# A two-layer state-space and expert kernel: order of TensorE's work in 28 of 47 expert tiles, and expert weights in three transfers

## The chip, the cores and the metric

One Trainium2 chip, one core of it. The metric is the device time of one execution in microseconds (us); less is better. The core's engines are TensorE (PE in the profile, its weight loads PEld), VectorE (DVE), ScalarE (ACT), GpSimd (POOL) and SyncE (SP, which here only issues transfers).

## The reference

`x` is 4 batches of 512 tokens with 512 channels. Two layers follow each other; each has a mixing part and a feed-forward part, both added to `x` with a gate:

```python
x = x + tanh(g_xattn[0]) * _L0_xattn_ref(ctx_1024, _layernorm(x), ...)   # state-space scan
x = x + tanh(g_ffn[0])   * _L0_ffn_ref(_layernorm(x), ...)               # 16 experts, 4 per token
x = x + tanh(g_xattn[1]) * _L1_xattn_ref(ctx_1024, _layernorm(x), ...)   # state-space scan
x = x + tanh(g_ffn[1])   * _L1_ffn_ref(_layernorm(x), ...)               # linear layer with low-rank experts
```

The scan keeps 16 states for each of 512 channels and goes along the 512 positions of a batch:

```python
state = state * exp(d[..., None] * A) + (d * u)[..., None] * b[:, None, :]
y = einsum('bdn,bn->bd', state, c)
```

The first layer's feed-forward part is a mixture of experts: `acc + we * (silu(x @ g.T) * (x @ u.T) @ d.T)` over 16 experts, where `g` and `u` are 256x512, `d` is 512x256 and `we` is zero for all but 4 experts of a token; a shared expert of the same shape is added. Everything is float32.

## The kernel before, in words

**Stages.** There are 8 scan stages `s`, one per layer and batch. Each has 32 units (16 states, each for two halves of the channels). A unit `k` is: ACT makes the decay (`exp`, L712), DVE multiplies (`mul_b`, L1702) and scans (L1710), POOL multiplies by C (`mul_c`, L457), and the result is summed; in stages 5 to 7 the sum is DVE's (`add_y`, L1721). The scan of the second layer does not need the first layer's output except at its end, so the expert work of the first layer is laid beside stages 5, 6 and 7 (`FIRST_B` = 5).

**Expert tiles.** The routed tokens are gathered in 47 tiles (`NTILE`), each for one expert: 32 full ones of 256 rows and 15 half ones of 128 rows (`KINDS`: tile `j` is half where `j % 3 == 1` and `j > 1`). Each of stages 5 to 7 has 16 turns (`TPS`) of two scan units, and a turn carries one tile. Turn `n` of stage `s` carries tile `j = 16 * (s - 5) + n - 1`, so tiles 0 to 14 lie in stage 5, 15 to 30 in stage 6 and 31 to 46 in stage 7. In stages 5 and 6 the turns with `n` up to 8 also carry the next stage's projection and convolution on PE (banks 4 and 5, `PRE`), and the turns up to 15 its softplus on ACT and DVE.

**One tile** has these steps: POOL gathers its rows (`gather_rows`, two turns ahead); PE transposes them (`tile_transposes`, L1164, halves `h` = 0 and 1); ACT copies them to `XST` (`tile_rows`, L762; one buffer for all tiles); PE makes gate and up products for two halves of the inner size (`tile_in`, L1185, `it` = 0 and 1, 16 matmuls each, banks 0 and 1); ACT takes the silu (`tile_silu`, L769), DVE multiplies (`tile_hidden`, L1728, which releases `h_ready`); PE multiplies by the down weights (`tile_out`, L1196, `it` = 0 and 1); ACT copies the result to `YSB` (`tile_out` of ACT, L776; one buffer for all tiles); SP stores it (`store_tile`, L341). Before the change the transposes write banks 0 and 1 as well, so half `h` of tile `j + 1` waits for DVE to have read half `h` of tile `j`.

**Orders written out by hand.** Every engine runs its list in order. In a turn with tile `j`:

- PE: products of `j` (both halves), then transposes of `j + 1` half 0, output of `j` half 0, transposes of `j + 1` half 1, output of `j` half 1, then the next stage's piece.
- ACT: decay, silu of `j` half 0, copy of tile `j - 1`'s output to `YSB`, silu of `j` half 1, the two row copies of `j + 1`, decay.
- DVE: hidden of `j` half 0, `add_y`, `mul_b`, hidden of `j` half 1, scan, `add_y`, `mul_b`, scan, then the next stage's piece.
- SP, turn `m` (the turn of tile `m - 1`): the B and C rows of a coming pair of units (`load_pair`, L316), the 1536 KB of weights of tile `m + 1` (`load_tile_w`, L335, into slot `(m + 1) % 2`), the store of tile `m - 1` (L341).

The waits that matter here, in SP's and ACT's lists:

```python
sp.wait_ge(mulc_done, HS * s + i * HPT + 2 * u + PRE_MULC - HPT + 2)   # load_pair: POOL's last turn
if j >= 2: sp.wait_ge(y_done, DONE[j - 1])                              # load_tile_w: tile j - 2 is out
sp.wait_ge(yev, DONE[j + 1])                                            # store_tile: ACT has copied tile j
act.wait_ge(ys_stored, j * 16)                                          # ACT's copy of j: tile j - 1 is stored
```

and in `mul_c` on POOL the wait `mulb_done, k + 2`: the multiplication of unit `k` by C waits for DVE's `mul_b` of unit `k + 1`.

Of the kernel before, what the change touches and what calls it, by code (L numbers as in the profile page):

```python
# [25 lines left out]
P = 128  # L26
# [6 lines left out]
INNER = 256  # L33
# [36 lines left out]
def build(nc, t):  # L70
    with ExitStack() as ctx:
# [86 lines left out]

        XT = lambda j: (PS[:, 0:2] if j else PS[:, 4:6]).rearrange("p a (k r) -> p a k r", k=ET // 2)
        GU = lambda j, it: PS[:, it if j else 4 + it]  # L160
# [17 lines left out]
        xs_in = [sem(f"xs_in{i}") for i in range(2)]  # L178
        tw_in = [sem(f"tw_in{i}") for i in range(2)]
        ys_stored, out_stored = sem("ys_stored"), sem("out_stored")  # L180
# [39 lines left out]
        def dt_bank(s, et):  # L220

            return (PRE[0], AUX[0])[et % 2] if s == FIRST_B else pre_bank(s, et)

        def rows_of(j):
# [71 lines left out]
        def _(sp):  # L296
# [32 lines left out]

            def load_tile_w(j, slot):  # L330
                if j >= 2:
                    sp.wait_ge(y_done, DONE[j - 1])
                at = expert_at(j)
                e = sp.value_load(TE[0:1, at:at + 1], min_val=0, max_val=NE - 1)
                sp.dma_start(MW[:, slot, :], t["moe_w"][bass.ds(e, 1), :, :].rearrange("a p n -> p (a n)")  # L335
                             ).then_inc(tw_in[slot], 16)

# [36 lines left out]
            for k in range(HS):  # L374
                load_unit(NB, k)
                if k == HPT + 1:
                    load_ctx(NB + 2)
                if k == 2 * HPT - 1:
                    sp.wait_ge(xn_ready, QT * NB)
                    sp.dma_start(xn_t[NB - 1], XN).then_inc(xn_stored, 16)  # L380
                if k == HS - 4:
                    sp.wait_ge(slots_ready, 2)
                    sp.wait_ge(shdown_done, QT * NB)
                    load_tile_w(0, 0)

            def tile_turn(s, i):
                for u in range(BODY):
# [10 lines left out]
                    if m == 0:  # L398
                        sp.wait_ge(scan_done, HS * FIRST_B + PRE_SCAN)
                        sp.wait_ge(indexed, ROUNDS)  # L400
                    if m + 1 < NTILE:
                        load_tile_w(m + 1, (m + 1) % 2)
                    if m:
                        store_tile(m - 1)

# [3 lines left out]
            for s in range(FIRST_B, STAGES):  # L409
                for i in range(TURNS):  # L410
                    if i == TURNS - 1 and s + 2 < STAGES:
                        load_ctx(s + 2)
                    tile_turn(s, i)

            sp.wait_ge(y_done, DONE[NTILE])
            for i in range(2):
                sp.wait_ge(tw_in[i], 16 * ((NTILE - i) // 2))
            sp.dma_start(BW, t["base_wT"].rearrange("(k p) n -> p k n", p=P)).then_inc(ld_ffn1, 16)
# [587 lines left out]
        def _(pe):  # L1006
# [128 lines left out]
            def shared_in(b, it):  # L1135
# [5 lines left out]
                for g in range(2):  # L1141
                    for k in range(ET):
                        at = g * WGU + k * INNER + it * P
                        mm = nc.tensor.matmul(AUX[g], MW[:, 0, at:at + P], XNT[:, k, :], start=(k == 0), stop=(k == ET - 1))  # L1144
# [11 lines left out]
            def tile_transposes(j, h):  # L1156

                pe.wait_ge(xs_in[j % 2], rows_in(j))
                if j:
                    pe.wait_ge(h_ready, (j - 1) * 2 + h + 1 + PRE_H)  # L1160
# [14 lines left out]

            def tile_in(j):
                u, n = j, P * BLOCKS[j]
                pe.wait_ge(tw_in[u % 2], 16 * (j // 2 + 1))
                pe.wait_ge(xst_ready, 2 * j + 2)
                for it in range(IT):  # L1180
                    pe.wait_ge(h_ready, j * 2 + (it - 1 + PRE_H))
                    for g in range(2):
                        for k in range(ET):
                            at = g * WGU + k * INNER + it * P
                            mm = nc.tensor.matmul(GU(j, it)[:, g * TILE:g * TILE + n], MW[:, u % 2, at:at + P],  # L1185
                                                  XST[:, k, 0:n], start=(k == 0), stop=(k == ET - 1))
                    mm.then_inc(gu_done, 1)

            def tile_out(j, it):
                u = j  # L1190
                pe.wait_ge(h_ready, j * 2 + (it + 1 + PRE_H))
                for r in range(BLOCKS[j]):
                    if it == 0 and DONE[j] + r >= 2:
# [122 lines left out]
            def tile_turn(s, i, prep):  # L1316
                p = s + 1
                for u in range(BODY):
                    n = i * BODY + u
                    j = TPS * (s - FIRST_B) + n - 1  # L1320
                    if j < 0:
                        continue
                    tile_in(j)
                    if j == 0:

                        pe.wait_ge(y4_ready, 1)
                        pe.wait_ge(scan_done, HS * FIRST_B + PRE_SCAN)
                    for it in range(IT):
                        if j < NTILE - 1:
                            tile_transposes(j + 1, it)  # L1330
                        tile_out(j, it)
                    if prep:
# [707 lines left out]
def _layouts(a):  # L2040
# [16 lines left out]
    def packed(gate, up, down):  # L2057

        n = gate.shape[0]
        rows = [w.transpose(0, 2, 1).reshape(n, ET, P, INNER).transpose(0, 2, 1, 3).reshape(n, P, WGU) for w in (gate, up)]  # L2060
        rows.append(down.transpose(0, 2, 1).reshape(n, IT, P, D).transpose(0, 2, 1, 3).reshape(n, P, IT * D))
# [29 lines left out]
```

## Time and profile before

| what | value |
|---|---|
| median of 3 runs | 1507.28 us (1506.95 to 1507.31) |
| the profiled execution's own time | 1501.42 us |
| its span (first to last instruction) | 1499.7 us |
| PE busy | 1261.5 us, 84% |
| DVE busy | 1353.0 us, 90% |
| ACT busy | 971.4 us, 65% |
| POOL busy | 784.2 us, 52% |
| granted TensorE clock | 0.952 of full |
| expert products (L1185) | 1504 matmuls, 284.1 us |
| expert outputs (L1196) | 316 matmuls, 156.2 us |
| weights of a tile | 48 transfers of 1536 KB, 9.1 us from issue to landing |

"Busy" adds up an engine's own instructions, and the engines work side by side, so the shares do not add up to 100%. The span is shorter than the time because the time also holds what lies before the first and after the last instruction. The stages of the expert tiles lie at 786 to 1333 us of the span.

### The profile page before, as it was taken

Reading aid. Unit: us, or ns where it says so; the run is one execution under the profiler, and the core shown is the slowest. Engines: PE = TensorE matmul, PEld = TensorE weight load, DVE = VectorE, ACT = ScalarE, POOL = GpSimd, SP = SyncE. Lnnn points to the kernel's source line nnn. Section 1 sums busy time; section 2 is a strip of 40 time slices with the busy share of each in tenths; the row PEclk is TensorE's granted clock in tenths of the full one; section 3 lists DMA queues with packets and bytes.
Section 4 is the critical chain, followed back from the end, with each engine's and each line's share of the span. In section 5 each row is a group of like instructions: output and inputs, shape, how many; then the busy total and the mean of one; then the engine's idle time right before and its main releaser. Section 6 shows DMA issues by size and latency. Waiting matters only on the chain. (4 is left out here: it accounts for less than half of the span.)

```text
span 1499.7 us, 14543 instructions
## 1 busy us (share of the span) xinstructions
PE 1261.5 (84%) x4518; PEld 721.7 (48%) x4518; DVE 1353.0 (90%) x1319; ACT 971.4 (65%) x1528; POOL 784.2 (52%) x411
## 2 busy tenths in 40 slices
PE   7785796899699868996989998899988899826998
PEld 3331242443244324442556666566666666615555
DVE  4999999998999899988898988999899999888894
ACT  5766568575864666625866788767887767734442
POOL 0465566545555553550465555555565665565632
PEclk9799999999999998998899999999999999977999
DMA  7444545535544443450356678677777887755531
GB/s 254 109 141 127 126 141 142 154 98 151 133 146 124 127 127 109 126 154 2 99 181 233 239 260 291 230 272 239 254 275 230 286 273 273 270 183 147 167 100 57
DMA packets 99837, 264.31 MB, mean 176 GB/s; under 512 B 10832, under 2 KB 11344, under 8 KB 93616
## 3 DMA queue, kind: packets, MB, share of 16 engines
q1 hardware_dynamic: 87936, 225.36, 48.4%
q0 software_dynamic: 11440, 37.50, 7.7%
q8 instruction: 36, 0.59, 0.2%
q10 hardware_dynamic: 384, 0.52, 0.1%
q14 instruction: 41, 0.34, 0.1%
HBM read 233.73 MB, written 29.62 MB: 176 GB/s over the span
## 5 line engine op out<-in xcount | busy, mean ns | idle before, releaser
L457 POOL TENSOR_TENSOR state<-state,bc_rows 128x1024 f32<-128x1024 f32 x254 | 599.2, 2359 | 613.6 <-DVE banks L1702 613.5
L1095 PE MATMUL banks<-state,ident 128*128 128x512 f32 x640 | 323.7, 638 | 106.6 <-POOL state L457 106.6
L1710 DVE TENSOR_TENSOR_SCAN state<-decay,banks 128x1024 f32<-128x1024 f32 x176 | 402.0, 2284 | 11.4 <-DVE banks L1702 5.0
L1702 DVE TENSOR_TENSOR banks<-du,bc_rows 128x1024 f32<-128x1024 f32 x256 | 314.5, 1229 | 13.4 <-DVE state L1710 0.5
L1185 PE MATMUL banks<-z_gate,expert_w 128*128 128x256 f32 (+1 forms) x1504 | 284.1, 347 | 7.5 <-DMA expert_w<-in_moe_w 7.5
L1185 PEld LDWEIGHTS banks<-z_gate,expert_w 128*128 128x128 f32 x1504 | 248.8, 191 | 60.1 <-issue 18.9
L1095 PEld LDWEIGHTS banks<-state,ident 128*128 128x128 f32 x640 | 118.0, 197 | 282.0 <-POOL state L457 170.0
L712 ACT ACTIVATE decay<-delta,neg_a 128x511 f32<-128x511 f32 x352 | 226.4, 710 | 16.8 <-DVE state L1710 11.6
L1710 DVE TENSOR_TENSOR_SCAN state<-expert_w,banks 128x1024 f32<-128x1024 f32 x80 | 182.9, 2286 | 6.9 <-ACT expert_w L712 4.2
L1196 PE MATMUL banks<-expert_w,hidden 128*128 128x512 f32 x316 | 156.2, 610 | 2.3 <-ACT expert_out L776 1.2
L1721 DVE TENSOR_TENSOR y_scan<-y_scan,state 128x1024 f32<-128x1024 f32 x94 | 114.3, 1216 | 3.6 <-POOL state L457 2.0
L712 ACT ACTIVATE expert_w<-delta,neg_a 128x511 f32<-128x511 f32 x160 | 104.1, 711 | 8.5 <-DVE state L1710 6.9
L762 ACT ACTIVATE z_gate<-banks 128x512 f32<-128x512 f32 (+1 forms) x94 | 49.6, 529 | 76.1 <-PE banks L1164 75.5
L712 ACT ACT_TABLE_LOAD x65 | 83.4, 1283 | 1.6 <-ACT x_dbl L578 0.4
L769 ACT ACTIVATE hidden<-banks 128x256 f32<-128x256 f32 (+1 forms) x94 | 33.2, 353 | 61.3 <-PE banks L1185 60.8
L1196 PEld LDWEIGHTS banks<-expert_w,hidden 128*128 128x128 f32 x316 | 54.8, 198 | 34.5 <-issue 31.2
L1728 DVE TENSOR_TENSOR hidden<-hidden,banks 128x256 f32<-128x256 f32 (+1 forms) x94 | 35.1, 373 | 32.6 <-ACT hidden L769 31.9
L1144 PE MATMUL banks<-y_scan,expert_w 128*128 128x512 f32 x128 | 59.0, 615 | 5.0 <-DVE hidden L1736 5.0
L769 ACT ACT_TABLE_LOAD x47 | 60.3, 1283 | 0.8
L1046 PE MATMUL banks<-ones,ident 128*128 128x128 f32 x274 | 36.1, 290 | 28.4 <-DVE neg_mean_rstd L1933 28.4
L1353 PE MATMUL banks<-expert_w,du 128*128 128x512 f32 x128 | 55.6, 592 | 0.0
L1016 PE MATMUL banks<-ctx_t,in_w 128*128 128x512 f32 x96 | 47.3, 641 | 9.6 <-DMA ctx_t<-in_ctxT 7.3
(318 smaller groups left out, 1659.2 us busy)
## 6 DMA issues: line engine op xcount, KB each, us to landing
bc_rows<-bc_d SPq DMA_DIRECT2D x208, 512.0 KB
expert_w<-in_moe_w SPq DMA_DIRECT2D x48, 1536.0 KB, 9.1
ys_d<-expert_out SPq DMA_DIRECT2D x32, 512.0 KB, 5.4
ctx_t<-in_ctxT SPq DMA_DIRECT2D x8, 512.0 KB, 6.7
x_res<-in_x SPq DMA_DIRECT2D x4, 1024.0 KB, 10.7
xn_d<-y_scan SPq DMA_DIRECT2D x4, 1024.0 KB, 7.7
ys_d<-expert_out SPq DMA_DIRECT2D x15, 256.0 KB, 5.9
out_x<-x_res SPq DMA_DIRECT2D x3, 1024.0 KB, 6.0
```

Of the source, the lines that this page charges most:

```text
L457: nc.gpsimd.tensor_tensor(W[:, c % 4], W[:, c % 4], bcast2(BC[:, u, 1, :]), ALU.mult).then_inc(mulc_done, 1)
L712: ins = nc.scalar.activation(DAS[c % n][:, m, 1:], DEL[:, s % 2, et, 1:], ACT.Exp, scale=AN[:, lay(s), et, state:state + 1])
L762: nc.scalar.activation(XST[:, 2 * h:2 * h + 2, 0:n], XT(j)[:, h, :, 0:n], ACT.Copy).then_inc(xst_ready, 1)
L769: nc.scalar.activation(HT[:, j % 2, it, 0:n], GU(j, it)[:, 0:n], ACT.Silu).then_inc(sil_ready, 1)
L1095: mm = nc.tensor.matmul(PS[:, m], ID[:, :], W[:, c % 4, m, :], start=False, stop=True, skip_group_check=True)
L1144: mm = nc.tensor.matmul(AUX[g], MW[:, 0, at:at + P], XNT[:, k, :], start=(k == 0), stop=(k == ET - 1))
L1185: mm = nc.tensor.matmul(GU(j, it)[:, g * TILE:g * TILE + n], MW[:, u % 2, at:at + P], XST[:, k, 0:n], start=(k == 0), stop=(k == ET - 1))
L1196: mm = nc.tensor.matmul(out_bank(j, r), HT[:, u % 2, it, r * P:(r + 1) * P], MW[:, u % 2, at:at + D], start=(it == 0), stop=(it == IT - 1))
L1353: nc.tensor.matmul(PS[:, q], xnt[:, q, k * P:(k + 1) * P], BW[:, k, :], start=(k == 0), stop=(k == ET - 1))
L1702: nc.vector.tensor_tensor(drive(s), DU[:, s % 2, 2 * h:2 * h + 2, :], bcast2(BC[:, u, 0, :]), ALU.mult).then_inc(mulb_done, 1)
L1710: nc.vector.tensor_tensor_scan(flat(W[:, c % 4]), flat(DAS[c % da_slots(s, i)]), flat(drive(s)), 0.0, ALU.mult, ALU.add).then_inc(scan_don ...
L1721: nc.vector.tensor_tensor(y, y, W[:, k % 4], ALU.add).then_inc(w_free, 1)
```

## The change

It does three things. (1) For tiles where `apart(j)` holds, PE's transposes write banks 4 and 5 instead of 0 and 1 and no longer wait for `h_ready`; these are tiles 10 to 16, 26 to 31 and 32 to 46, 28 in all, at times when the next stage's projection does not use these banks. (2) For these tiles both transposes come first and the first products (`it` = 0) are issued between the two output halves of the tile before. (3) The weights are laid out by inner half and loaded for all tiles in three transfers of 512 KB with a semaphore each: the `it` = 0 products, the `it` = 1 products, the down weights. The first two wait for `gu_done` of tile `j - 2` in place of its `y_done`. In SP's turn `m` this gives the order: pair rows, part 0 of tile `m + 1`, part 2 of tile `m`, store of tile `m - 2`, part 1 of tile `m + 1`.

```diff
-        XT = lambda j: (PS[:, 0:2] if j else PS[:, 4:6]).rearrange("p a (k r) -> p a k r", k=ET // 2)
+        XT = lambda j: (PS[:, 4:6] if j == 0 or apart(j) else PS[:, 0:2]).rearrange("p a (k r) -> p a k r", k=ET // 2)
-        tw_in = [sem(f"tw_in{i}") for i in range(2)]
+        tw_in = [[sem(f"tw_in{i}_{part}") for part in range(IT + 1)] for i in range(2)]
+        def apart(j):
+            s, n = FIRST_B + j // TPS, j % TPS
+            return 0 < j < NTILE and (s == STAGES - 1 or n == 0 or n >= 10)
-            def load_tile_w(j, slot):
-                if j >= 2:
-                    sp.wait_ge(y_done, DONE[j - 1])
+            def load_tile_w(j, parts):
                 at = expert_at(j)
                 e = sp.value_load(TE[0:1, at:at + 1], min_val=0, max_val=NE - 1)
-                sp.dma_start(MW[:, slot, :], t["moe_w"][bass.ds(e, 1), :, :].rearrange("a p n -> p (a n)")
-                             ).then_inc(tw_in[slot], 16)
+                for part in parts:
+                    if j >= 2 and part < IT:
+                        sp.wait_ge(gu_done, (j - 2) * 2 + part + 1)
+                    elif j >= 2:
+                        sp.wait_ge(y_done, DONE[j - 1])
+                    lo = part * WGU
+                    sp.dma_start(MW[:, j % 2, lo:lo + WGU], t["moe_w"][bass.ds(e, 1), :, lo:lo + WGU].rearrange(
+                        "a p n -> p (a n)")).then_inc(tw_in[j % 2][part], 16)
...
                     if m == 0:
                         sp.wait_ge(scan_done, HS * FIRST_B + PRE_SCAN)
                         sp.wait_ge(indexed, ROUNDS)
+                    if m == 0:
+                        load_tile_w(1, range(IT + 1))
+                        continue
                     if m + 1 < NTILE:
-                        load_tile_w(m + 1, (m + 1) % 2)
-                    if m:
-                        store_tile(m - 1)
+                        load_tile_w(m + 1, (0,))
+                    if 2 <= m < NTILE:
+                        load_tile_w(m, (IT,))
+                    if m >= 2:
+                        store_tile(m - 2)
+                    if m + 1 < NTILE:
+                        load_tile_w(m + 1, (1,))
...
+            store_tile(NTILE - 1)
...
                 pe.wait_ge(xs_in[j % 2], rows_in(j))
-                if j:
+                if apart(j):
+                    pe.wait_ge(dt_read, ET * min(STAGES, FIRST_B + 1 + -(-j // TPS)))
+                    pe.wait_ge(xst_ready, 2 * j)
+                elif j:
                     pe.wait_ge(h_ready, (j - 1) * 2 + h + 1 + PRE_H)
...
-            def tile_in(j):
+            def tile_in(j, it):
                 u, n = j, P * BLOCKS[j]
-                pe.wait_ge(tw_in[u % 2], 16 * (j // 2 + 1))
                 pe.wait_ge(xst_ready, 2 * j + 2)
-                for it in range(IT):
...
+                pe.wait_ge(tw_in[u % 2][it], 16 * (j // 2 + 1))
+                pe.wait_ge(h_ready, j * 2 + (it - 1 + PRE_H))
...
             def tile_out(j, it):
                 u = j
                 pe.wait_ge(h_ready, j * 2 + (it + 1 + PRE_H))
+                pe.wait_ge(tw_in[u % 2][IT], 16 * (j // 2 + 1))
...
-                    tile_in(j)
+                    if not apart(j):
+                        tile_in(j, 0)
+                    tile_in(j, 1)
...
-                    for it in range(IT):
-                        if j < NTILE - 1:
-                            tile_transposes(j + 1, it)
-                        tile_out(j, it)
+                    if apart(j + 1):
+                        for h in range(2):
+                            tile_transposes(j + 1, h)
+                        tile_out(j, 0)
+                        tile_in(j + 1, 0)
+                        tile_out(j, 1)
+                    else:
+                        for it in range(IT):
+                            if j < NTILE - 1:
+                                tile_transposes(j + 1, it)
+                            tile_out(j, it)
```

The shared expert reads the same new layout (`shared_in`), and the host packs the weights to match (`packed`). ACT's, DVE's and POOL's lists are not touched.

## Rows read from the trace of the kernel before

**Rows 1.** Windows view, stage 7: length, busy us (instructions) by engine, clock, DMA share, GB/s

```profile
1155.00:1328.00 173.00, 151.35 (x714) 111.20 (x713) 159.41 (x132) 122.41 (x188) 101.46 (x55) 0.99 0.78 257
```

**Rows 2.** Waits of DVE, 1160.6 to 1321.5: us in total, times, longest

```profile
DVE hidden L1728 <- ACT hidden L769: 9.6, 16, 1.2
DVE state L1710 <- DVE banks L1702: 1.9, 3, 0.6
```

**Rows 3.** Waits of PE, 1155 to 1328

```profile
PE banks L1185 <- DMA expert_w<-in_moe_w: 6.0, 5, 1.8
```

**Rows 4.** Waits of DVE in 786:907, 907:978, 978:1092 and 1092:1155

```profile
DVE hidden L1728 <- ACT hidden L769: 8.4, 10, 1.8
...
DVE hidden L1728 <- ACT hidden L769: 3.4, 4, 1.1
...
DVE hidden L1728 <- ACT hidden L769: 7.1, 10, 2.1
...
DVE hidden L1728 <- ACT hidden L769: 3.0, 2, 2.0
```

**Rows 5.** Timeline of DVE: first hidden of tiles 9, 16, 25, 31 and 46

```profile
901.84 0.42 DVE L1728 TENSOR_TENSOR hidden<-hidden,banks 128x256 f32<-128x256 f32 x1 [1.52 <-ACT hidden L769]
...
983.29 0.26 DVE L1728 TENSOR_TENSOR hidden<-hidden,banks 128x128 f32<-128x128 f32 x1
...
1089.74 0.29 DVE L1728 TENSOR_TENSOR hidden<-hidden,banks 128x128 f32<-128x128 f32 x1 [1.37 <-ACT hidden L769]
...
1160.57 0.28 DVE L1728 TENSOR_TENSOR hidden<-hidden,banks 128x128 f32<-128x128 f32 x1
...
1321.58 0.29 DVE L1728 TENSOR_TENSOR hidden<-hidden,banks 128x128 f32<-128x128 f32 x1 [0.42 <-ACT hidden L769]
```

**Rows 6.** Timeline of DVE in stage 7: both hiddens of tile 32, first of 33

```profile
1171.14 0.40 DVE L1728 TENSOR_TENSOR hidden<-hidden,banks 128x256 f32<-128x256 f32 x1
...
1173.72 0.41 DVE L1728 TENSOR_TENSOR hidden<-hidden,banks 128x256 f32<-128x256 f32 x1
...
1181.30 0.42 DVE L1728 TENSOR_TENSOR hidden<-hidden,banks 128x256 f32<-128x256 f32 x1 [0.26 <-ACT hidden L769]
```

**Rows 7.** Timeline of all engines, 1201 to 1208: tile 35, store of 34, next pair rows

```profile
1202.04 0.42 DVE L1728 TENSOR_TENSOR hidden<-hidden,banks 128x256 f32<-128x256 f32 x1 [0.50 <-ACT hidden L769]
...
1202.53 0.33 SPq L341 DMA_DIRECT2D ys_d<-expert_out  x1
...
1204.89 2.35 POOL L457 TENSOR_TENSOR state<-state,bc_rows 128x1024 f32<-128x1024 f32 x1 [2.04 <-DVE banks L1702]
...
1207.27 0.37 SPq L316 DMA_DIRECT2D bc_rows<-bc_d  x1
```

**Rows 8.** Timeline of SP: pair rows, then weights with no wait between

```profile
1262.82 0.36 SPq L316 DMA_DIRECT2D bc_rows<-bc_d  x1
...
1263.95 0.66 SPq L335 DMA_DIRECT2D expert_w<-in_moe_w  x1
```

**Rows 9.** Issue to landing: L341 in 1155:1328, L341 in 786:1155, L335 at 1263.95

```profile
DMA to landing us min/median/max: 2.2/6.5/8.5
...
DMA to landing us min/median/max: 2.5/5.5/7.1
...
DMA to landing us min/median/max: 9.7/9.7/9.7
```

**Rows 10.** Timeline of ACT, tile 36: copies of tile 35 to YSB, second silu

```profile
1213.73 1.08 ACT L776 ACTIVATE expert_out<-banks 128x512 f32<-128x512 f32 x2
1216.30 0.38 ACT L769 ACTIVATE hidden<-banks 128x256 f32<-128x256 f32 x1 [1.49 <-PE banks L1185]
```

**Rows 11.** Timeline of PE: four transposes after a long and after a short wait

```profile
949.85 1.09 PE L1164 MATMUL banks<-ident,z_gate 128*128 128x128 f32 x4 [4.85 <-DVE hidden L1728]
...
1192.19 0.63 PE L1164 MATMUL banks<-ident,ctx_t 128*128 128x128 f32 x4 [1.06 <-DVE hidden L1728]
```

**Rows 12.** Timeline of PE: the 32 product matmuls of full tile 36

```profile
1209.19 7.07 PE L1185 MATMUL banks<-z_gate,expert_w 128*128 128x256 f32 x32
```

More of the change, by code:

```diff
@@ L383, in _ @@
                     sp.wait_ge(shdown_done, QT * NB)
-                    load_tile_w(0, 0)
+                    load_tile_w(0, range(IT + 1))
             def tile_turn(s, i):
@@ L413, in _ @@
                     tile_turn(s, i)
+            store_tile(NTILE - 1)
             sp.wait_ge(y_done, DONE[NTILE])
             for i in range(2):
-                sp.wait_ge(tw_in[i], 16 * ((NTILE - i) // 2))
+                for part in range(IT + 1):
+                    sp.wait_ge(tw_in[i][part], 16 * ((NTILE - i + 1) // 2))
             sp.dma_start(BW, t["base_wT"].rearrange("(k p) n -> p k n", p=P)).then_inc(ld_ffn1, 16)
@@ L1142, in shared_in @@
                     for k in range(ET):
-                        at = g * WGU + k * INNER + it * P
+                        at = it * WGU + (g * ET + k) * P
                         mm = nc.tensor.matmul(AUX[g], MW[:, 0, at:at + P], XNT[:, k, :], start=(k == 0), stop=(k == ET - 1))
@@ L1174, in index_round @@
                 mm.then_inc(indexed, 1)
-            def tile_in(j):
+            def tile_in(j, it):
                 u, n = j, P * BLOCKS[j]
-                pe.wait_ge(tw_in[u % 2], 16 * (j // 2 + 1))
                 pe.wait_ge(xst_ready, 2 * j + 2)
-                for it in range(IT):
[L1181 to L1187, printed above, removed]
+                pe.wait_ge(tw_in[u % 2][it], 16 * (j // 2 + 1))
+                pe.wait_ge(h_ready, j * 2 + (it - 1 + PRE_H))
+                for g in range(2):
+                    for k in range(ET):
+                        at = it * WGU + (g * ET + k) * P
+                        mm = nc.tensor.matmul(GU(j, it)[:, g * TILE:g * TILE + n], MW[:, u % 2, at:at + P],
+                                              XST[:, k, 0:n], start=(k == 0), stop=(k == ET - 1))
+                mm.then_inc(gu_done, 1)
             def tile_out(j, it):
@@ L2059, in packed @@
         n = gate.shape[0]
-        rows = [w.transpose(0, 2, 1).reshape(n, ET, P, INNER).transpose(0, 2, 1, 3).reshape(n, P, WGU) for w in (gate, up)]
+        both = [w.transpose(0, 2, 1).reshape(n, ET, P, IT, P).transpose(0, 2, 3, 1, 4) for w in (gate, up)]
+        rows = [np.stack(both, axis=3).reshape(n, P, 2 * WGU)]
         rows.append(down.transpose(0, 2, 1).reshape(n, IT, P, D).transpose(0, 2, 1, 3).reshape(n, P, IT * D))
```

## The prediction

> **What bounds the kernel now.** I began with the windows view of stage 7, where 15 of the 28 changed tiles lie, to see whether one engine is full there. DVE is busy for 159.41 of 173 us and PE for 151.35, with the DMA engines at 0.78 [rows 1]: DVE is the limit with 13.6 us of holes, and PE is close behind. The waits view names the holes: DVE stood 9.6 us in 16 waits for ACT's silu before a hidden product, and 1.9 us before a scan [rows 2]. PE in turn stood 6.0 us for weights [rows 3]. The same wait of DVE takes 3.4 and 3.0 us where the other changed tiles lie, 8.4 and 7.1 us where the unchanged ones lie [rows 4]. Last I read the timeline as a clock of turns: the first hidden of tile 31 starts at 1160.57 and that of tile 46 at 1321.58, so a turn of stage 7 takes 161.0 / 15 = 10.73 us; without the 11.5 us of waits it would take 9.97. For tiles 9 to 16 it is 11.6 us, for 16 to 25 and for 25 to 31 it is 11.8 [rows 5]. Within a turn the second hidden comes 2.58 us after the first, and the next turn's first one 7.32 us after that when its wait of 0.26 is taken off [rows 6].
>
> **What the change removes.** Transposes in banks 4 and 5 no longer wait for DVE's read of banks 0 and 1, so ACT's row copies, the decay and the next silu come earlier; the first products no longer stand behind the last output half; and each third of the weights is asked for a tile earlier or has a tile longer to land, so the 6.0 us of rows 3 go. All of this ends in one place, the wait of DVE for the silu. If nothing new came, I would count the waits of DVE in the changed tiles: 11.5 in stage 7, 3.4 + 3.0 before, in all 17.9 us. PE has room for it, since its work in rows 1 is 8 us less than DVE's. The number of matmuls, transposes, copies and scans stays as it is, and the transposes' own reordering costs nothing: they are the same instructions on the same engine.
>
> **What it adds on SP.** Each turn has two more register loads and two more weight transfers. SP is not full, but its list is in order, and here I see the cost. Call 0 the first hidden of tile m - 1. Before, SP already stood at the store of tile m - 2 and issued it at 0.49 (1202.53 against 1202.04). Only then came the pair rows of the next turn, and they waited for POOL's `mul_c`, which itself waits for DVE's next `mul_b`: 1207.27, that is 5.23 [rows 7]. After the change the store of tile m - 2 stands behind these pair rows and behind two of the three weight parts. From pair rows to a weight transfer without any wait takes 1.13 us, the register load included [rows 8]. So the store is issued at 5.23 + 1.13 + 1.13 + 0.4 (one issue, 0.37 in rows 7) = 7.9, over 7 us later than now.
>
> **Who waits for that.** `YSB` is one buffer, and ACT's copy of tile m - 1 waits until the store of tile m - 2 has landed. Behind that copy stand, on ACT, the second silu of tile m, both row copies of tile m + 1, and the decays; DVE's scan waits for the second hidden, which waits for that silu.
>
> **When does the store land?** The trace does not show this order, so I bound it. A store takes 6.5 us at the median of stage 7 [rows 9], which gives 14.4; the earlier stages' median of 5.5 gives 13.4 as the low end. From above: pair rows plus 1536 KB of weights are 2 MB, as much as pair rows, two weight parts and the store will be, and they landed 1.13 + 9.7 = 10.8 us after the pair rows were issued [rows 8, 9], which gives 5.23 + 10.8 = 16.1; a store at the maximum of 8.5 gives 16.4. I take 15.2, the middle of 14.4 and 16.1: the store will have more bytes just ahead of it than it has today.
> The Trainium skill, "DMA: Bandwidth & Descriptors", section "Queues, rings and completion order", says that each DMA engine takes the descriptors of one issuer's ring in the order in which they were put there. By that rule alone the upper figure, 16.1, would be the one to use, and the sum below would grow by about 7 us in stage 7.
>
> **The new loop.** After landing, ACT copies the tile (1.08 us) and takes the silu (0.38) [rows 10]: the second hidden of tile m starts at 15.2 + 1.5 = 16.7 at the earliest. It is due 2.58 after the first one of tile m, so a turn is held by what the turn before it lacks of 14.1 us. From this hidden to the next turn's first one are 7.32 us. Two turns thus take at least 16.7 + 7.3 = 24.0 us, 12.0 each; whether long and short turns alternate or all are equal, the mean is the same.
>
> **The sum.**
> - Stage 7: (12.0 - 10.73) x 15 turns = +19 us. This holds the removed waits already. Ends: 13.4 gives 22.2 for two turns, +6; 16.4 gives 25.2, +28.
> - Changed tiles of stages 5 and 6: 13 turns of 11.7, of which 6.4 / 13 = 0.5 go as waits, base 11.2. Stores land 1.0 us sooner there [rows 9], so the threshold is 13.1 and the mean (11.2 + 13.1) / 2 = 12.15: 0.45 x 13 = +6. Ends: at 13.4 landing, threshold 12.3, the mean is 11.75, about +1; a landing of 15.4 there gives a threshold of 14.3, a mean of 12.75 and +14.
> - Unchanged tiles: they get the new SP order too. 18 turns of 11.8 give (11.8 + 13.1) / 2 = 12.45, at most +12; but here DVE has 15.5 us of waits for PE [rows 4] that the hold replaces rather than adds to. I take +4, ends 0 and +12.
> - The two more transfers, the new layout and the last tiles' order: 0, as SP stands idle at its waits and all three weight parts have more than a turn to spare; should that cover go, a part would be late as the weights are in rows 3, 6 us in all of stage 7.
>
> Together +29 us, with ends at +7 and +54. Against the profiled execution's own time, 1501.4, this gives 1530; the median of the runs is 5.9 us above that execution, and so I forecast 1536.
>
> **Rivals.**
> *No hold, faster.* If the store lands soon enough, the holes go and nothing takes their place: -17.9 us, 1489. The point from which it decides is in the loop: two turns as long as today's, 21.46 us, leave 21.46 - 7.32 - 1.5 - 7.9 = 4.7 us from issue to landing. For it: one store landed in 2.2 us [rows 9], the last, with nothing before it in the queue. Against it: the medians of 5.5 and 6.5, and that 1.5 MB now go ahead of the store. At a landing of 4.0 us stage 7 would gain 6 and the rest 6, 1495. Chance 0.17.
> The Trainium skill, same page, section "Anatomy of one DMA — SWDGE (gpsimd) path", fits 2.0 us plus bytes at 436 GB/s. By this estimate 2 MB would be there 6.8 us after the pair rows and the loop would be 20.8 us, so the change would come out slightly faster, about 1495; rows 9, with 9.7 us for 1.5 MB alone, do not agree. The same page advises at least 1 MiB for each transfer, which speaks against the split in any case.
>
> *Near zero.* A landing around 4.7 us, the two effects cancel, 1507. Chance 0.05.
>
> *Hold and a slow PE.* While ACT is held, PE has its transposes and one output half behind it and waits for the row copies, up to 5 us in a turn. After a wait of 4.85 us four transposes took 1.09 us, after one of 1.06 they took 0.63 [rows 11]: the clock was granted at its lower level, 1.2 GHz instead of 2.4. Sixteen product matmuls take 7.07 / 2 = 3.5 us [rows 12] and would take 7.0. In the forecast I hold this covered, because at 12.0 us a turn PE has over 1 us to spare. Uncovered it adds 1 to 2 us to each turn of stage 7, 15 to 30 us: 1551 to 1566. Chance 0.12.
>
> The forecast's own case has 0.66.
>
> **How the numbers follow.** The likeliest case gives 1536, its own ends being 1514 and 1561. To hold 8 of 10 the range reaches up through the slow PE to 1566 and down to 1497, into the quicker landings; what is left out is most of the no-hold case. A measurement of this kernel tells about 0.2%, 3 us, from no change. Slower by more: forecast and slow PE, 0.78; within: 0.05; faster: 0.17.
>
> **What would show it.** In the profile after: the store (L341) issued some 8 us after the first hidden of the tile before, with its landing 5 to 8 us later; ACT idle before its copy L776 on a transfer of `ys_d`, about 2 us in each turn of stage 7, a group that is missing now; DVE waiting before the second hidden, not the first; the PE waits of rows 3 gone; 12 us from one first hidden to the next in stage 7. I am wrong if L776 does not wait: then stage 7 should run at 10 us a turn. I am also wrong if the wait is there but another engine has taken the bound, which a DVE wait on decay or bc_rows would show.

## The result, and the profile after

The changed kernel takes 1569.74 us (median of 6 runs, 1565.75 to 1576.18) against 1507.3 us: the ratio is 1.0406 with a 95% interval of 1.0377 to 1.0436. It is slower, as forecast, but by 62 us where 29 were forecast, and outside the range of 1497 to 1566. The profiled execution took 1566.63 us with a span of 1564.9.

The windows view has the same columns as [rows 1]: length, busy us (instructions) by engine, granted clock, DMA share, GB/s. The three stretches are tiles 9 to 16, tiles 16 to 25 (unchanged ones) and stage 7.

```profile
912.00:1001.40 89.40, 72.30 (x322) 52.35 (x320) 77.58 (x65) 63.92 (x94) 48.46 (x25) 0.90 0.67 231
1001.40:1128.40 127.00, 113.11 (x448) 75.29 (x448) 96.28 (x86) 79.30 (x123) 58.94 (x35) 0.89 0.64 210
1205.70:1388.20 182.50, 152.31 (x672) 111.60 (x672) 146.40 (x122) 113.35 (x178) 105.72 (x53) 0.93 0.72 239
```

No engine is full in stage 7 any more: DVE has 36 us of holes where [rows 1] had 13.6, and PE 30. TensorE's granted clock fell from 0.99 to 0.93, and to 0.89 over the unchanged tiles 16 to 25. Something other than an engine sets the pace. Three rows of the costliest groups name it; behind the second bar is the idle time ahead of the group and what ended most of it:

```profile
L1221 PE MATMUL banks<-expert_w,hidden 128*128 128x512 f32 x316 | 168.8, 649 | 74.3 <-ACT expert_out L797 70.5
L797 ACT ACTIVATE expert_out<-banks 128x512 f32<-128x512 f32 x79 | 43.7, 595 | 153.3 <-DMA ys_d<-expert_out 152.0
L1763 DVE TENSOR_TENSOR hidden<-hidden,banks 128x256 f32<-128x256 f32 (+1 forms) x94 | 34.9, 371 | 101.7 <-ACT hidden L790 101.6
```

ACT's copy (L797) stands 152 us for the store of the tile before; the group had no such wait before. DVE's first read of the silu (L1763) stands 101.6 us, and PE's output matmuls (L1221) stand 70.5 us for ACT's copy. That last wait was 1.2 us before, and the prediction does not have it.

The timeline of one turn of stage 7 shows the forecast loop. Columns: start, duration, instruction, and in brackets the idle time before it with its releaser.

```profile
1279.04 0.26 DVE L1763 TENSOR_TENSOR hidden<-hidden,banks 128x128 f32<-128x128 f32 x1
...
1283.79 1.08 ACT L797 ACTIVATE expert_out<-banks 128x512 f32<-128x512 f32 x2 [5.88 <-DMA ys_d<-expert_out]
...
1284.53 2.05 PE L1221 MATMUL banks<-expert_w,hidden 128*128 128x512 f32 x2 [5.14 <-ACT expert_out L797]
...
1285.07 0.29 DVE L1763 TENSOR_TENSOR hidden<-hidden,banks 128x128 f32<-128x128 f32 x1 [3.35 <-ACT hidden L790]
1285.09 0.38 SPq L322 DMA_DIRECT2D bc_rows<-bc_d  x1
...
1286.23 1.79 SPq L346 DMA_DIRECT2D expert_w<-in_moe_w  x2
...
1288.07 0.43 SPq L352 DMA_DIRECT2D ys_d<-expert_out  x1
1289.26 0.34 SPq L346 DMA_DIRECT2D expert_w<-in_moe_w  x1
```

SP issues the pair rows (L322) 6.05 us after the first hidden (1279.04), then two weight parts (L346), and only then the store (L352), 9.0 us after that hidden. The median of all turns is 7.9; in stage 7 eight of 14 stores have 8.7 to 9.0. Its landing, as issue to landing in the view of that one line (first in stage 7, then in the stages before it; [rows 9] had 6.5 and 5.5):

```profile
DMA to landing us min/median/max: 4.4/7.6/8.8
...
DMA to landing us min/median/max: 6.8/7.7/9.3
```

The length of a turn, from first hiddens as in [rows 5] (before, after, and what the stretch lost):

| tiles | before | after | lost, us |
|---|---|---|---|
| 0 to 9, unchanged | 12.05 | 13.08 | 9.3 |
| 9 to 16 | 11.64 | 12.77 | 8.0 |
| 16 to 25, unchanged | 11.83 | 14.11 | 20.5 |
| 25 to 31 | 11.80 | 12.88 | 6.4 |
| 31 to 46 (stage 7) | 10.73 | 12.17 | 21.6 |

Of the 66 us almost half, 29.8, were lost in tiles whose PE order the change does not touch. Within these, the loss is uneven: the turn of tile 22 takes 20.2 us for 10.4 before, that of tile 19 takes 16.9 for 11.9, and the two make 14.8 of the 20.5 us of their stretch.

The same timelines show where in a turn the unchanged tiles lose (means, in us):

| tiles | first to second hidden, before | after | second to next first, before | after |
|---|---|---|---|---|
| 0 to 9 | 2.95 | 4.05 | 9.10 | 9.03 |
| 16 to 25 | 2.88 | 4.47 | 8.95 | 9.64 |

So 24.2 of the 29.8 us are lost before the second hidden, and nearly all of the rest in the turn of tile 22.

### The profile page after: what moved, and what is told of

It is laid out like the page before. It is cut to its first block, busy times and chain, and to the rows that moved or that the text cites. A ratio compares the mean times of both kernels' runs of the same rounds, so it can differ in the third digit from the quotient of the medians.

```text
span 1564.9 us, 15192 instructions
## 1 busy us (share of the span) xinstructions
PE 1291.2 (83%) x4518; PEld 737.8 (47%) x4518; DVE 1351.4 (86%) x1319; ACT 968.4 (62%) x1528; POOL 795.6 (51%) x411
## 4 chain that ended last, share of the span: by engine, by line
PE 28%; DVE 26%; DMA 11%; POOL 8%; ACT 7%; issue 6%; SPq 2%; DVEq 0%; ACTq 0%; POOLq 0%
DVE state L1745 11%; DMA ys_d<-expert_out 10%; DVE banks L1737 8%; POOL state L478 5%; PE banks L1116 5%; PE banks L1209 5%; PE banks L1221 3%; PE banks L1388 3%; PE banks L1165 2%; PE banks L1060 2%; PE banks L1173 2%; PE banks L1037 1%; ACT L733 1%; ACT decay L733 1%; DVE y_scan L1756 1%
## 5 line engine op out<-in xcount | busy, mean ns | idle before, releaser
L1737 DVE TENSOR_TENSOR banks<-du,bc_rows 128x1024 f32<-128x1024 f32 x256 | 314.5, 1229 | 13.4 <-DVE state L1745 0.5
L1209 PE MATMUL banks<-z_gate,expert_w 128*128 128x256 f32 (+1 forms) x1504 | 302.9, 358 | 3.4 <-ACT z_gate L783 2.9
L1209 PEld LDWEIGHTS banks<-z_gate,expert_w 128*128 128x128 f32 x1504 | 261.1, 198 | 79.3 <-issue 28.4
L733 ACT ACTIVATE decay<-delta,neg_a 128x511 f32<-128x511 f32 x352 | 226.4, 710 | 15.4 <-DVE state L1745 11.7
L1221 PE MATMUL banks<-expert_w,hidden 128*128 128x512 f32 x316 | 168.8, 649 | 74.3 <-ACT expert_out L797 70.5
L797 ACT ACTIVATE expert_out<-banks 128x512 f32<-128x512 f32 x79 | 43.7, 595 | 153.3 <-DMA ys_d<-expert_out 152.0
L1763 DVE TENSOR_TENSOR hidden<-hidden,banks 128x256 f32<-128x256 f32 (+1 forms) x94 | 34.9, 371 | 101.7 <-ACT hidden L790 101.6
L1221 PEld LDWEIGHTS banks<-expert_w,hidden 128*128 128x128 f32 x316 | 56.9, 203 | 114.3 <-issue 97.5
L733 ACT ACTIVATE expert_w<-delta,neg_a 128x511 f32<-128x511 f32 x160 | 104.1, 711 | 8.5 <-DVE state L1745 6.9
L783 ACT ACTIVATE z_gate<-banks 128x512 f32<-128x512 f32 (+1 forms) x94 | 47.9, 541 | 24.5 <-PE banks L1189 24.2
L493 POOL DMA_INDIRECT z_gate<-xn_d,selected x40 | 54.3, 1357 | 8.4 <-issue 5.6
```

Source lines behind the costliest of these rows:

```text
L493: nc.gpsimd.indirect_dma_start(out=rows_of(j)[:, r, :], out_offset=None, in_=xn_d, in_offset=bass.IndirectOffsetOnAxis(ap=IDX[:, at:at + 1 ...
L733: ins = nc.scalar.activation(DAS[c % n][:, m, 1:], DEL[:, s % 2, et, 1:], ACT.Exp, scale=AN[:, lay(s), et, state:state + 1])
L1221: mm = nc.tensor.matmul(out_bank(j, r), HT[:, u % 2, it, r * P:(r + 1) * P], MW[:, u % 2, at:at + D], start=(it == 0), stop=(it == IT - 1))
L1737: nc.vector.tensor_tensor(drive(s), DU[:, s % 2, 2 * h:2 * h + 2, :], bcast2(BC[:, u, 0, :]), ALU.mult).then_inc(mulb_done, 1)
```

## The experiments

All are written as SP's order in turn `m`. W0, W1, W2 are the three weight parts. Before: pair rows, all weights of `m + 1`, store of `m - 1`. Changed: pair rows, W0 of `m + 1`, W2 of `m`, store of `m - 2`, W1 of `m + 1`. Every ratio is against the kernel before, on the same chip.

**1. The store back to its old place.**

```diff
-                    if m >= 2:
-                        store_tile(m - 2)
                     if m + 1 < NTILE:
                         load_tile_w(m + 1, (1,))
+                    store_tile(m - 1)
```

> The changed kernel with one thing put back: SP stores tile m - 1 at the end of turn m, as the kernel before did, and not tile m - 2 between the weight parts. If the late store is the whole loss, ACT's copy no longer waits for ys_d, and the waits of DVE for the silu go in the changed tiles: 17.9 us under before, near 1489 us, stage 7 at 10 us a turn. Rival (the new order on PE or the three transfers cost by themselves): part of the 62 us stays, over 1507 us.

Measured: 1523.84 us, ratio 1.008 (1.0054 to 1.0107). ACT's wait for `ys_d` is gone, and the time falls by 46 us. But the kernel stays slower than before, where 1489 us were expected. What holds it now, in PE's waits (us in total, times, longest; "issue" names no releaser, and experiment 6 tests the reading):

```profile
PE banks L1219 <- issue: 19.4, 7, 4.5
...
PE banks L1219 <- DMA expert_w<-in_moe_w: 9.6, 3, 4.7
```

and in the timeline of stage 7:

```profile
1239.52 1.78 SPq L346 DMA_DIRECT2D expert_w<-in_moe_w  x2
...
1246.36 1.20 PE L1219 MATMUL banks<-expert_w,hidden 128*128 128x512 f32 x2 [3.19 <-issue]
```

W2 is issued in the turn in which it is used, and 6.8 us later PE's output matmuls start, having stood 3.19 us. The prediction gave every part more than a turn to spare; the down weights have less than one.

**2. Only the store moved late.** The kernel before, in which SP's `store_tile(m - 1)` becomes `store_tile(m - 2)`; nothing else is changed.

> The kernel before with one thing moved: SP stores tile m - 2 behind the weights of turn m instead of tile m - 1. Here the weights still wait for the outputs of tile m - 1 and are 1.5 MB ahead of the store. Late-store theory: issued 8.6 us after the first hidden, landed near 18.7, so two turns take 18.7 + 1.5 + 7.3 = 27.5 us, 13.75 a turn in stage 7 (+45 us) and about as much in stages 5 and 6: 1590 to 1620 us. Rival (PE's order is the loss): no change, 1507 us.

Measured: 1644.32 us, ratio 1.089 (1.0844 to 1.0937). A turn takes 14.2 to 14.7 us in every stretch. The waits of ACT and of PE:

```profile
ACT expert_out L777 <- DMA ys_d<-expert_out: 198.1, 44, 7.5
...
PE banks L1197 <- ACT expert_out L777: 116.8, 39, 6.9
```

This is above what I expected (1590 to 1620; 2 runs) and over twice what the whole change costs; here the store stands behind one transfer of 1536 KB and the wait of that transfer. It also shows the wait of PE for the copy, without any of the change's new PE order.

**3. and 4. The parts alone, the order alone.** Both start from experiment 1. Experiment 3 has PE's old order:

```diff
         def apart(j):
-            return 0 < j < NTILE and (s == STAGES - 1 or n == 0 or n >= 10)
+            return False
```

Experiment 4 has the new order and one transfer of 1536 KB that waits for `y_done`, as before.

> The first experiment without PE's new order: three weight transfers, store as before, apart() false for every tile. The 6.0 us that PE waited for weights in stage 7 go. Theory that this wait lay on the path: 3 to 6 us under before, 1501 to 1504 us. Rival, hidden by the waits of DVE for hidden products: no change, 1507 us.

> The first experiment without the split: PE's new order, store as before, one weight transfer per tile that waits for the outputs of tile j - 2. The load is issued 0.9 us after those outputs and lands 9.2 us later, and the first products behind it now stand ahead of the next outputs: 0.9 + 9.2 + 3.5 + 1.7 = 15.3 us from output to output of full tiles, about 14.8 on average against 10.7 to 11.8 in the 28 changed tiles: near 1600 us. Rival (the split is needed only for a few us): below 1510 us.

Measured: experiment 3, 1530.74 us, ratio 1.0135 (1.0104 to 1.0165), where 1501 to 1504 us were expected. Experiment 4, 1564.56 us (2 runs), ratio 1.0362 (1.0313 to 1.0411), where near 1600 were expected, and its largest wait of PE in this part is the one at its first products, 76.4 us in 28 waits:

```profile
PE banks L1198 <- issue: 76.4, 28, 5.8
```

In the new order the first products of `m` come before the last output half of `m - 1`, and the single transfer for `m + 1` waits for that half, so it is issued later and wanted earlier: the order needs the split. The row names no releaser; in the timeline of 1240 to 1316 us the products that waited start 6.8 to 8.7 us after the transfer's issue, whose median to landing is 8.2. And the split with W2 late costs 1.35% under the old order too.

**5. W2 early, the store still late.** Pair rows, W0 and W1 of `m + 1`, store of `m - 2`, W2 of `m + 1`.

> The changed kernel with the down weights a turn earlier: SP's turn m is pair rows, parts 0 and 1 of tile m + 1, store of tile m - 2, part 2 of tile m + 1. The store keeps its place, 7.9 us after the first hidden, with two weight parts ahead. Theory that in the changed kernel the late store binds before the late down weights: 1560 to 1570 us, 12 us a turn in stage 7. Rival, the down weights (issued 7.5 us after the first hidden, 6.9 us to land, wanted near 10.5 us) carry part of the 62 us there: 1530 to 1550 us.

Measured: 1574.5 us (2 runs), ratio 1.0425 (1.0359 to 1.049), a little over the 1560 to 1570 expected and the same as the changed kernel; ACT waits 145.7 us for `ys_d`. In the changed kernel the late W2 is hidden behind the late store.

**6. Both early.**

```diff
                     if m + 1 < NTILE:
                         load_tile_w(m + 1, (0,))
-                    if 2 <= m < NTILE:
-                        load_tile_w(m, (IT,))
-                    if m >= 2:
-                        store_tile(m - 2)
-                    if m + 1 < NTILE:
                         load_tile_w(m + 1, (1,))
+                        load_tile_w(m + 1, (IT,))
+                    store_tile(m - 1)
```

> Store as in the kernel before and down weights of tile m + 1 in turn m: pair rows, parts 0, 1 and 2 of tile m + 1, store of tile m - 1. Theory that what was left in the first experiment is PE waiting before its outputs for down weights that are asked for a turn late: the wait before L1221's first matmul goes; part 0 is now tight (issued at 6.3 us, 6.9 us to land, wanted at 12.2 us), so up to 1 us a turn in stage 7 may stay: 1489 to 1500 us. Rival, the three transfers cost on the DMA engines by their number: stays near 1524 us.

Measured: 1496.29 us, ratio 0.9905 (0.9872 to 0.9939). With two late issues mended the change is a gain; stage 7 takes 10.42 us a turn.

**7. and 8. A sequence of my own, with the new and the old PE order.** Pair rows, W2 of `m + 1`, store of `m - 1`, W0 and W1 of `m + 2`; experiment 8 also has `apart` false.

> Every weight part in the first place its slot is free: SP's turn m is pair rows, part 2 of tile m + 1, store of tile m - 1, parts 0 and 1 of tile m + 2. Each part now has over 4 us to spare. If nothing but the places on SP was wrong with the change, the 17.9 us of the first estimate come out: 1489 us, 10 us a turn in stage 7. Rival as in the run before: number of transfers, over 1500 us.

> The run before without PE's new order (apart() false for all tiles): what well placed thirds of the weights are worth alone. PE's waits for weights (6.0 us in stage 7, 7.5 us in all) go, the waits for hidden products stay: 1501 to 1505 us. The difference to the run before is what PE's new order is worth: 12 to 16 us by the waits of DVE.

Measured: 1493.29 us, ratio 0.989 (0.9851 to 0.993), and 1501.88 us, ratio 0.9947 (0.9925 to 0.9969). So of 16.5 us the well-placed split is worth 8 and PE's order 8.6, less than the 12 to 16 expected. Stage 7 takes 10.31 us a turn, 0.34 above the 9.97 that the prediction gave without waits. DVE's waits in experiment 7 show two remainders, the silu (none of it in stage 7) and POOL's `mul_c`:

```profile
DVE hidden L1760 <- ACT hidden L787: 18.6, 22, 2.1
...
DVE y_scan L1753 <- POOL state L475: 10.4, 12, 1.0
```

**9. The late store with a second buffer.** Experiment 5 with two places for ACT's copy and a semaphore for each, so that the copy of tile `j` waits for the store of `j - 2`:

```diff
+        def ysb(j):
+            if j % 2 == 0:
+                return YSB
+            return Y[:, 3, 2:4] if j < 22 else INW
...
-                if j:
-                    act.wait_ge(ys_stored, j * 16)
+                if j > 1:
+                    act.wait_ge((ys_stored, ys_stored2)[j % 2], j // 2 * 16)
```

> e5_down_early_store_late with a second buffer for ACT's copy, so that the copy of tile m - 1 waits for the store of tile m - 3 and not of m - 2. The store is issued as late as in e5. If the one buffer is what turns the late store into time, the 145.7 us of ACT's waits for ys_d go (under 5 us left), PE's waits for ACT's copy go with them, and the time falls from 1574.5 to that of e6_both_early, 1496 (1488 to 1505). If instead the queue itself is late (its transfers hold everything else up, whoever waits), the time stays above 1540 and another transfer takes the place of ys_d among the waits.

Measured: 1495.56 us, ratio 0.9919 (0.9883 to 0.9956): 79 us less than experiment 5 by this one edit. Stage 7 takes 10.50 us a turn, ACT waits for no store there, and the stores still land late. Issue to landing, in the view of the store's line over stage 7:

```profile
DMA to landing us min/median/max: 2.8/7.9/9.4
```

The transfers are as slow as in the changed kernel, and issued as late. Only the wait on the single buffer turned that into time; the rival, a queue that is late for everybody, falls.

**10. The silu ahead of the held copy.** The changed kernel, with ACT's `tile_out(j - 1)` moved behind `tile_silu(j, 1)`. No other engine's list changes.

> The changed kernel, in which ACT takes the second silu of tile m ahead of the copy of tile m - 1. DVE's second hidden no longer stands behind the held copy through ACT's order; PE's next output half still does, through the two banks that the copy reads. Theory A, the path through ACT's order is what the held copy costs (as in my prediction): stage 7 falls from 12.17 to about 11.1 us a turn (16 us less) and the 27 us that tiles 0 to 9 and 16 to 25 were longer than before falls to under 10, in all 1530. Theory B, the path through PE's output banks carries it in the unchanged tiles: they keep 20 us or more of their 30, ACT's waits for ys_d stay over 100 us and PE's wait for the copy (70.5 us) grows to over 90; the time is 1550 to 1570.

Measured: 1561.13 us, ratio 1.0369 (1.0318 to 1.042). Two rows of waits:

```profile
ACT expert_out L797 <- DMA ys_d<-expert_out: 54.3, 22, 5.5
...
PE banks L1221 <- ACT expert_out L797: 70.0, 33, 6.0
```

The turns are 13.02 us in tiles 0 to 9, 13.07 in 16 to 25 and 11.97 in stage 7. Against before, the unchanged tiles still lose (13.02 - 12.05) x 9 + (13.07 - 11.83) x 9 = 19.9 us, and stage 7 gives back only 3 of its 21.6. The time is the one that theory B gave, but the run does not separate the two theories. Theory B wanted over 100 us in ACT's wait and over 90 in PE's; PE's is what it was in the changed kernel, 70.0 against 70.5. And DVE's waits only moved: in the unchanged tiles 6.5 us stand before the second hidden, against 28.7 in the changed kernel, but 20.9 before a scan, against 5.5. The row of that wait, and a turn without any wait for a store, tile 1 (the row copies, L783, and the decay, L733, stand behind the copy on ACT, and the scan needs the decay):

```profile
DVE state L1745 <- issue: 29.6, 18, 3.8
...
814.58 1.08 ACT L797 ACTIVATE expert_out<-banks 128x512 f32<-128x512 f32 x2
817.75 0.60 ACT L783 ACTIVATE z_gate<-banks 128x512 f32<-128x512 f32 x1 [1.59 <-PE banks L1189]
819.66 2.56 ACT L733 ACTIVATE decay<-delta,neg_a 128x511 f32<-128x511 f32 x4
821.08 2.29 DVE L1745 TENSOR_TENSOR_SCAN state<-decay,banks 128x1024 f32<-128x1024 f32 x1 [1.48 <-issue]
```

In 12 of the 18 unchanged turns ACT waits for no store, and these still make 8.5 of the 19.9 us. So the new place of the copy costs by itself, and the edit without the late store was not run. The share of the path through PE's banks stays open.

**11. The gather of the next rows split over POOL's two gaps.** Experiment 7 with one `indirect_dma_start` after each `mul_c`.

> e7_resequenced with POOL's gather of the next pair rows split, one row block after each mul_c, where e7 issues both after one mul_c. In e7 DVE waited 10.4 us in 12 waits for a mul_c that came late behind the two gathers, and turns with the gathers in front took 10.66 us against 9.81. If that is the cause, DVE's wait for mul_c goes below 3 us, stage 7 takes 9.8 to 10.0 us a turn and the time is 1486 (1482 to 1491). If the gather's issues cost the same wherever they stand, no change: 1493.

Measured: 1509.35 us (12 runs), ratio 1.0011 (0.9988 to 1.0034). This was a miss: 16 us slower than experiment 7 instead of 7 faster. DVE's 10.4 us wait for `mul_c` did go. But the second row block is now asked for half a turn later, and PE's transposes wait for it. PE's waits in 1160 to 1320:

```profile
PE banks L1188 <- DMA ctx_t<-xn_d,selected: 10.1, 4, 4.7
PE banks L1188 <- DMA z_gate<-xn_d,selected: 5.1, 3, 2.3
```

Experiment 7 has no such wait there. It is the mistake of the change on another queue: a transfer moved behind other work, with no look at who waits for its landing.

**12. The store late in the unchanged tiles only.** Experiment 6, with the store of `m - 2` between W1 and W2 in turns 3 to 10 and 18 to 26, and the store of `m - 1` at the end of all turns but 2 to 9 and 17 to 25.

> e6_both_early (1496.3) with the store issued late, as in the changed kernel, only in the turns of the unchanged tiles (2 to 9 and 17 to 25), 17 turns. My prediction gave such turns +4 us in all, ends 0 and +12: 1500 (1496 to 1508). The profile of the changed kernel says that they lost 29.8 us of the stretches 0 to 9 and 16 to 25: then 1526 (1520 to 1532), with stage 7 unchanged at 10.4 us a turn and ACT's waits for ys_d at 50 to 80 us.

Measured: 1527.07 us, ratio 1.0123 (1.0084 to 1.0163), with stage 7 at 10.47 us a turn and 46.4 us of ACT's waits for `ys_d`, a little under the 50 expected. Against experiment 6, tiles 0 to 9 take 13.56 us for 11.97 and tiles 16 to 25 13.49 for 11.84, so (1.59 + 1.65) x 9 = 29 us come from these two stretches, as the profile of the changed kernel had it. The prediction gave them +4. The sum agrees with the 29.8 of the changed kernel, the split does not: 14.3 and 14.9 here, 9.3 and 20.5 there. Of the 29 us, 17.0 are lost between first and second hidden and 11.2 behind the second one in the turns of tiles 7 and 22, where PE's work takes longer as in tile 22 of the changed kernel (below). The late stores also reach into the tiles behind them, as tiles 9 to 16 lose 4.9 us and 25 to 31 4.8.

## Why the prediction was right in direction and wrong in size

**Right: the mechanism.** The store was forecast at 7.9 us after the first hidden and is issued at 7.9 at the median of all turns. ACT's copy does wait for `ys_d`, and the weight waits of [rows 3] are gone. Experiment 9 shows that the single `YSB` is what makes the late store cost anything.

**Right, with errors that partly cancel: stage 7.** ACT's held copies start 16.2 us (median) after the first hidden of the turn before, where I took 15.2 for the landing: the store is issued later than forecast in most turns, and lands 7.6 us later. By the prediction's own loop that gives 16.2 + 1.5 + 7.3 = 25.0 us for two turns, 12.5 each; 12.17 were measured, 12.0 forecast. So what follows the landing is shorter than in the loop: from a second hidden to the next first are 7.15 us, and the output of a half tile is one copy, not two. The term of +19 came out at +21.6. As forecast, DVE's waits in stage 7, 35.4 us, all stand before the second hidden. ACT's wait is 66.7 us there, 4.4 a turn where 2 were forecast.
The Trainium skill, "DMA: Bandwidth & Descriptors", section "Queues, rings and completion order", says that each DMA engine takes the descriptors of a ring in order, which by the prediction's reading meant 16.1; the 16.2 of stage 7 agree, and the 15.6 measured in the unchanged tiles lie between that and the value taken.
Section "Anatomy of one DMA — SWDGE (gpsimd) path" of the same page, for transfers that GpSimd issues, fits 2.0 us plus bytes at 436 GB/s, which gave 6.8 us for the 2 MB; here the 512 KB store alone needed 7.7, so this rival was rightly held small.

**Wrong, and the failed step: the unchanged tiles.** The step reads "here DVE has 15.5 us of waits for PE that the hold replaces rather than adds to. I take +4". They lost 29.8 us in the changed kernel, and experiment 12 gets 29 by the late store there alone. Part of this is the same landing: the upper end of +12, worked out with 14.5 (15.6 + 1.5 - 2.6) for the threshold of 13.1, is (11.8 + 14.5) / 2 = 13.15 a turn and 1.35 x 18 = +24. But the value taken was wrong by its reason, that the hold takes the place of the old wait.

The step took the waits of [rows 4] for one wait. They are two. In the turns of tiles 0 to 9 and 16 to 25 the trace before has 7.3 us in front of a tile's first hidden and 5.3 in front of its second. The held copy delays the second silu, so it could take the place of the 5.3 only. After the change 28.7 us stand in front of the second hidden and 13.4 in front of the first: nothing was replaced. The 24.2 us lost between first and second hidden lie on the path through ACT's list that the prediction followed, and are what its own form gives without the discount (+24).

The step also left out who waits for the copy on the other side: PE's next output half writes the two banks that the copy reads. PE's wait for it in tiles 0 to 9 and in tiles 16 to 25 of the changed kernel:

```profile
PE banks L1221 <- ACT expert_out L797: 5.1, 4, 2.1
...
PE banks L1221 <- ACT expert_out L797: 11.5, 4, 5.1
```

That is 16.6 of the 70.5 us; what it adds to the time is not shown by any run. PE has little room here: the windows view of experiment 6, where no copy is held, has for tiles 16 to 25 and for stage 7 (columns as above):

```profile
980.30:1086.90 106.60, 103.13 (x448) 70.69 (x448) 96.28 (x86) 78.19 (x121) 59.22 (x35) 0.98 0.78 255
...
1154.40:1310.70 156.30, 145.84 (x672) 108.89 (x672) 146.66 (x123) 112.58 (x173) 105.82 (x53) 0.98 0.83 274
```

PE is busy for 97% of tiles 16 to 25. The changed kernel's row of the same tiles has the same 448 matmuls at 113.11 us and a clock of 0.89: PE's own work takes 10.0 us more in a stretch that is 20.4 longer. In tiles 0 to 9 the clock stayed at 0.99, and 9.3 us were lost all the same. The timeline of tile 22, the longest turn, shows both paths:

```profile
1087.39 1.09 ACT L797 ACTIVATE expert_out<-banks 128x512 f32<-128x512 f32 x2 [4.85 <-DMA ys_d<-expert_out]
...
1088.13 2.05 PE L1221 MATMUL banks<-expert_w,hidden 128*128 128x512 f32 x2 [3.70 <-ACT expert_out L797]
...
1089.69 0.29 DVE L1763 TENSOR_TENSOR hidden<-hidden,banks 128x128 f32<-128x128 f32 x1 [4.55 <-ACT hidden L790]
...
1090.13 1.09 PE L1189 MATMUL banks<-ident,y_scan 128*128 128x128 f32 x4
...
1092.85 3.78 PE L1099 MATMUL banks<-x_dbl,dt_w 16*128 16x512 f32 x4
...
1102.39 0.38 ACT L790 ACTIVATE hidden<-banks 128x256 f32<-128x256 f32 x1 [5.37 <-PE banks L1209]
...
1102.81 0.42 DVE L1763 TENSOR_TENSOR hidden<-hidden,banks 128x256 f32<-128x256 f32 x1 [5.93 <-ACT hidden L790]
```

DVE's second hidden stands 4.55 us behind the held copy. PE is held 3.70 us by the copy, then does its transposes, the next layer's products and the first expert products one after another, and DVE's next first hidden waits 5.93 us at the end. The hold and the old wait stand one behind the other in the turn; neither replaces the other. The wait for the banks was hardly the later one here: the transposes at 1090.13 also need the second hidden, which ended at 1089.98, so without the wait for the banks they could have begun 0.15 us sooner. From these transposes to DVE's next first hidden are 12.7 us; experiment 6 has the same work in 7.5 (1054.02 to 1061.53), so 5.2 of the 9.8 us that this turn lost are PE's work at the lower clock. The "hold and a slow PE" rival had the second half of this: after the hold four transposes take 1.09 us, as in [rows 11]. It was priced for stage 7 alone, and as a clock effect with no wait of PE for a bank. Its 1551 to 1566 was near the result for a partly wrong reason.

**Wrong in size: changed tiles of stages 5 and 6,** +6 forecast and 14.4 measured, at the forecast's upper end. Their landing was taken 1.0 us shorter than in stage 7, from [rows 9]; after the change it is the same, 7.7 against 7.6. With 15.6 in place of 14.2 the prediction's own threshold becomes 15.6 + 1.5 - 2.6 = 14.5, the mean (11.2 + 14.5) / 2 = 12.85, and the term (12.85 - 11.7) x 13 = +15. So the form of the step held, and the landing was the mis-sized part.

**Wrong, without effect on the number: "all three weight parts have more than a turn to spare".** Experiments 1 and 3 show W2 late, for 0.8 and 1.35% of slowdown; experiment 5 shows that it costs nothing as long as the store is the later of the two.

**Right: the gain.** The 17.9 us of waits that the change should remove, had nothing new come, compare with 16.5 (1493.29) in experiment 7, 13.5 in experiment 6 and 12.8 in experiment 9; the intervals of the three overlap. The Trainium skill's advice of at least 1 MiB for each transfer, in the page named above, section "Bandwidth", did not decide anything here: in experiment 8 three transfers of 512 KB under the old PE order are 0.5% faster than one of 1536 KB.

**Open: the share of the lower clock.** Over the five stretches together PE is busy for 510.44 us in the changed kernel and for 482.39 in experiment 6, with 2161 and 2160 matmuls. So up to 28 us of the 62 may be the clock's, as a consequence of the holds; no run changed the clock alone, and not all of that work lies on the path. The 5.2 us in the turn of tile 22 do. In stage 7, which has 6.5 of these 28 us, ACT waited 2.6 us in all for PE before a silu.

## What to carry to other kernels

A transfer's place in an in-order issue queue is part of its data's path: before moving one, list who waits for its landing, and what in turn is held by that waiter, on every side of it (its engine's list, and the buffers it reads as well as those it writes). A single buffer with a copy-out behind it takes the full delay, and a second buffer took 79 us of it away here while the transfers stayed as late. Where the same late step hits stretches with different limits, price each with the engine that is tight there; an existing wait absorbs a new one only if both end at the same instruction.

## What the runs showed of the hardware that I had not expected

- **A transfer's size does not give its landing time.** In stage 7 the same 512 KB store lands in 6.5 us (median) before the change, in 7.6 in the changed kernel, in 7.9 in experiment 9 and in 4.6 in experiment 11. What the place in the queue does to it I did not measure by itself.
- **The work behind a wait of PE pays again.** The granted clock of tiles 16 to 25 fell from 0.98 to 0.89, and after a hold of 3.70 us PE ran at its lower level of 1.2 GHz for at least the next 8 us: the four `dt_w` matmuls that took 3.78 us in tile 22 take 1.98 in experiment 7:

```profile
1061.57 1.98 PE L1096 MATMUL banks<-x_dbl,dt_w 16*128 16x512 f32 x4
```

- **A gather issued half a turn later on POOL** turned a 10.4 us wait of DVE into a kernel 16 us slower (experiment 11), although no engine got more work.
